# A four-layer graph network on one core: all arithmetic moved off GpSimd, to ScalarE and VectorE

## What is computed

```python
x = layernorm(x + L0(x))   # relu(adj @ (f1 * (adj @ (x @ W1)))) , then the same with W2 and f2, no relu
x = layernorm(x + L1(x))   # [x, adj @ x] @ weight
m = x @ W_msg + b_msg;  gates = sigmoid((m @ W_q) @ (m @ W_k).T / sqrt(128) + gate_bias) * adj * adj
u = relu([x, gates @ m] @ W_upd + b_upd);  x = layernorm(x + (layernorm(u) * ln_gamma + ln_beta))
x = layernorm(x + L3(x))   # z = swish(adj @ z @ W + b), twice
```

## Time and profile before

| what | value |
|---|---|
| device time, median of 3 runs | 1895.87 us (1895.03 to 1899.65) |
| span of the profiled execution | 1896.7 us |
| PE / DVE / ACT / POOL busy | 1683.2 / 1494.3 / 1007.3 / 471.2 us |
| busy share of the span | 89% / 79% / 53% / 25% |
| chain that ended last | PE 51%, DVE 34%, issue 9%, ACT 2%, POOL 1% |
| read from HBM | 420 MB, mean 223 GB/s |

### The profile page before, as it was taken

The page is one execution under the profiler, slowest core; times in us unless marked ns, Lnnn a source line. Parts: engine busy times, 40 slices in busy tenths (PEclk is TensorE's granted clock), DMA queues, the critical chain, the costliest instruction groups (busy, mean ns, idle before and its releaser), DMA issues.

```text
span 1896.7 us, 18699 instructions
## 1 busy us (share of the span) xinstructions
PE 1683.2 (89%) x7618; PEld 776.0 (41%) x7618; DVE 1494.3 (79%) x1231; ACT 1007.3 (53%) x709; POOL 471.2 (25%) x187
## 2 busy tenths in 40 slices
PE   7999999999999899898978786786786879999986
PEld 4444444444444444444433342242232434444432
DVE  6874565537556974788999999999999997654997
ACT  5764455446445543655646654554554756553753
POOL 1000000000000210112475656756756140000022
PEclk9999999999999999999989988888888999999999
DMA  9986776647766756666723433333333679764983
GB/s 374 391 315 232 258 312 248 240 176 285 268 243 230 280 206 239 246 246 240 266 89 133 149 118 111 118 126 111 112 132 111 240 252 353 286 232 171 351 304 139
DMA packets 59206, 423.64 MB, mean 223 GB/s; under 512 B 6800, under 2 KB 6960, under 8 KB 8304
## 3 DMA queue, kind: packets, MB, share of 16 engines
q1 hardware_dynamic: 57888, 417.88, 59.8%
q0 software_dynamic: 1088, 4.49, 0.7%
q10 hardware_dynamic: 144, 0.07, 0.0%
HBM read 420.32 MB, written 2.10 MB: 223 GB/s over the span
## 4 chain that ended last, share of the span: by engine, by line
PE 51%; DVE 34%; issue 9%; ACT 2%; POOL 1%; DMA 1%; SPq 0%; POOLq 0%; DVEq 0%; ACTq 0%
PE acc L502 32%; PE spare L502 15%; DVE gates L867 10%; DVE a_lo L851 9%; DVE a_lo L843 7%; ACT a_hi L677 2%; DVE bn L773 2%; PE rows L415 1%; PE rows L408 1%; DMA a_ring<-adj_dram 1%; DVE stats L784 1%; POOL x_rows L918 1%; DVE stats L787 1%; PE rows L421 1%; DVE moments L776 1%
## 5 line engine op out<-in xcount | busy, mean ns | idle before, releaser
L843 DVE SCALAR_TENSOR_TENSOR a_lo<-a_ring,a_hi 128x2048 f16<-128x2048 f32 x332 | 777.3, 2365 | 308.2 <-ACT a_hi L677 307.8
L677 ACT ACTIVATE a_hi<-a_ring 128x2048 f16<-128x2048 f32 x332 | 630.0, 1907 | 419.1 <-PE spare L502 275.1
L502 PE MATMUL acc<-a_hi,y_hi 128*128 128x512 f16 x1584 | 488.1, 390 | 157.9 <-DVE a_lo L851 121.4
L502 PE MATMUL acc<-a_hi,y_lo 128*128 128x512 f16 x1584 | 489.8, 391 | 0.0
L502 PE MATMUL acc<-a_lo,y_hi 128*128 128x512 f16 x1584 | 489.5, 391 | 0.0
L957 POOL TENSOR_TENSOR a_ring<-a_ring 128x1024 f32<-128x1024 f32 x112 | 312.1, 2813 | 97.2 <-DMA a_ring<-adj_dram 97.2
L909 POOL TENSOR_TENSOR val<-val,moments 128x1024 f32<-128x1024 f32 x19 | 51.2, 2694 | 1027.6 <-DVE moments L776 1027.6
L502 PEld LDWEIGHTS acc<-a_hi,y_hi 128*128 128x128 f16 x1584 | 150.2, 99 | 367.6 <-DVE a_lo L851 153.5
L685 ACT ACTIVATE a_hi<-gates 128x1024 f16<-128x1024 f32 x128 | 135.2, 1056 | 246.1 <-DVE gates L867 246.1
L851 DVE TENSOR_TENSOR a_lo<-gates,a_hi 128x1024 f16<-128x1024 f32 x128 | 263.5, 2058 | 0.0
L867 DVE SCALAR_TENSOR_TENSOR gates<-gates,a_ring 128x1024 f32<-128x1024 f32 x128 | 258.6, 2021 | 0.0
(11 more groups left out here) (111 smaller groups left out, 979.3 us busy)
## 6 DMA issues: line engine op xcount, KB each, us to landing
a_ring<-adj_dram SPq DMA_DIRECT2D x396, 1024.0 KB, 5.1
x_T<-xt_dram SPq DMA_DIRECT2D x4, 512.0 KB, 8.1
x_rows<-x_dram POOLq DMA_DIRECT2D x1, 2048.0 KB, 10.6
out_dram<-x_rows POOLq DMA_DIRECT2D x3, 512.0 KB, 4.6
out_dram<-x_rows SPq DMA_DIRECT2D x2, 256.0 KB, 2.0
w<-W_dram POOLq DMA_DIRECT2D x2, 64.0 KB, 5.4
wcat<-Wcat_dram POOLq DMA_DIRECT2D x1, 128.0 KB, 7.0
wupd<-W_upd_dram POOLq DMA_DIRECT2D x1, 128.0 KB, 7.6
```

The source lines that it names most:

```text
L502: mm = pe.matmul(sums[:, h * BANK:(h + 1) * BANK], blk(y[:, y_pass % 2, :], j), slot(a, st)[:, s, h * BANK:(h + 1) * BANK], start=(begins ...
L677: act.activation(slot(a_hi, st), loaded(st), ACT.Copy, scale=2.0 ** A_EXP).then_inc(s_ahi, 1)
L843: dve.scalar_tensor_tensor(out=slot(a_lo, st).rearrange("p s c -> p (s c)"), in0=loaded(st).rearrange("p s c -> p (s c)"), scalar=2.0 ** A ...
```

## The change

- The squares: ScalarE squares a whole step (128 x 2048) in one instruction, `square`. The first is issued ahead of the first sigmoid, and then one for the next step behind the second unit of each step. GpSimd squares nothing, and there is no eighth block of ScalarE's.
- The high halves: for units with u % 8 in (1, 4, 6) VectorE writes the high half by `tensor_copy`, directly behind low(u-1). The other five of eight stay on ScalarE. The two engines count on semaphores of their own.
- The layer norms: VectorE subtracts and scales in one instruction per block of 128 x 128, eight per norm (`normalise_blocks`), right behind the Newton steps or one or two units later. The norm with gain and offset takes sixteen (`normalise_affine`).
- The last chunk's halves are normalised by VectorE, four instructions each.
- GpSimd keeps the initial fill of the identity, its loads and the three stores.

```diff
@@ -32,7 +32,7 @@
 GATED = 6
 AHEAD = 4
 LONE_LOGITS = 5
-ACT_SQUARES = 8
+HIGH_BY_VECTOR = (1, 4, 6)
 
 
 A_EXP = 10
...
@@ -332,6 +332,19 @@
 
         def gated_index(st, s):
             return (st.n - GATED_FROM) * SJ + s
+
+        def high_by_vector(u):
+
+            return u % 8 in HIGH_BY_VECTOR
+
+        def highs_by_vector(u):
+
+            return sum(high_by_vector(v) for v in range(u))
+
+        def slot_free(u):
+
+            before = STREAM[GATED_FROM + u // SJ - RING]
+            return LAST_USE[before.n] + 1 - (SJ - 1 - u % SJ if before.p == GATED else 0)
 
         def in_idle_sums(u):
 
@@ -677,12 +690,16 @@
                 act.activation(slot(a_hi, st), loaded(st), ACT.Copy, scale=2.0 ** A_EXP).then_inc(s_ahi, 1)
 
             def gate_high(u):
+                if high_by_vector(u):
+                    return
                 st = STREAM[GATED_FROM + u // SJ]
                 act.wait_ge(s_g, u + 1)
-
-                before = STREAM[st.n - RING]
-                act.wait_ge(s_unit, LAST_USE[before.n] + 1 - (SJ - 1 - u % SJ if before.p == GATED else 0))
-                act.activation(slot(a_hi, st)[:, u % SJ, :], gates[:, u % G_RING, :], ACT.Copy).then_inc(s_ghi, 1)
+                act.wait_ge(s_unit, slot_free(u))
+                act.activation(slot(a_hi, st)[:, u % SJ, :], gates[:, u % G_RING, :], ACT.Copy).then_inc(s_ghi_act, 1)
+
+            def square(st):
+                act.wait_ge(s_a[st.n % LOADS], 16 * (st.n // LOADS + 1))
+                act.activation(loaded(st), loaded(st), ACT.Square).then_inc(s_sq, 1)
 
             for st in STREAM:
                 if st.p != GATED:
@@ -692,9 +709,8 @@
                 for s in range(SJ):
                     u = gated_index(st, s)
                     at = epilogue(stages, at, FIRST_USE[st.n] + s - AHEAD + 1)
-                    if u % ACT_SQUARES == ACT_SQUARES - 1:
-                        act.wait_ge(s_a[st.n % LOADS], 16 * (st.n // LOADS + 1))
-                        act.activation(loaded(st)[:, s, :], loaded(st)[:, s, :], ACT.Square).then_inc(s_sqa, 1)
+                    if u == 0:
+                        square(st)
                     act.wait_ge(s_lg, u + 1)
                     if u >= G_RING:
 
@@ -706,6 +722,8 @@
                                    scale=2.0 ** -(Q_EXP + K_EXP) * F ** -0.5).then_inc(s_pr, 1)
                     if u >= 1:
                         gate_high(u - 1)
+                    if s == SJ - 1 and u < NB * NC - 1:
+                        square(STREAM[st.n + 1])
                     if u == NB * NC - 1:
                         gate_high(u)
             epilogue(stages, at, THE_END)
...
@@ -811,6 +829,32 @@
                     rstd_of(range(CB), CB * n, n)
                 return go
 
+            def normalise_blocks(blocks, dst, n):
+
+                dve.wait_ge(s_newton, 3 * NEWTON * n)
+                for b in blocks:
+                    op = dve.tensor_scalar(dst(b), val[:, b, :], moments[:, b, 0:1], stats[:, 1, b:b + 1], ALU.subtract,
+                                           ALU.mult)
+                op.then_inc(s_ln, 1)
+
+            def normalise(run):
+                def go(p, k):
+                    normalise_blocks(range(CB), lambda b: normalised(p, k, run)[:, b, :], nth("ln", p, k, run))
+                return go
+
+            def normalise_affine(p, k):
+
+                n = nth("ln", p, k, 0)
+                dve.wait_ge(s_newton, 3 * NEWTON * n)
+                for b in range(CB):
+                    dve.scalar_tensor_tensor(out=xn[:, b, :], in0=val[:, b, :], scalar=moments[:, b, 0:1], in1=gam[:, :],
+                                             op0=ALU.subtract, op1=ALU.mult).then_inc(s_scaled, 1)
+                for b in range(CB):
+                    dve.wait_ge(s_scaled, CB * (nth("resid", p, k) - 1) + b + 1)
+                    op = dve.scalar_tensor_tensor(out=xn[:, b, :], in0=xn[:, b, :], scalar=stats[:, 1, b:b + 1],
+                                                  in1=bet[:, :], op0=ALU.mult, op1=ALU.add)
+                op.then_inc(s_ln, 1)
+
             def qk_low(run, hi, lo, exp):
                 def go(p, k):
                     i = ORDER[p][k]
@@ -826,15 +870,16 @@
                 1: {0: [take_over], 1: [values], 2: [y_low]},
                 2: {0: [take_over], 2: [y_low]},
                 3: {0: [take_over], 1: [values], 2: [y_low]},
-                4: {0: [take_over], 1: [values, ln_moments(0, s_val, "val"), ln_rstd(0)], 5: [y_low]},
-                5: {0: [take_over], 1: [values], 2: [ln_moments(0, s_val, "val"), ln_rstd(0)],
+                4: {0: [take_over], 1: [values, ln_moments(0, s_val, "val"), ln_rstd(0), normalise(0)], 5: [y_low]},
+                5: {0: [take_over], 1: [values], 2: [ln_moments(0, s_val, "val"), ln_rstd(0), normalise(0)],
                     7: [qk_low(0, kT_hi, kT_lo, K_EXP)], 8: [qk_low(1, qT_hi, qT_lo, Q_EXP)], 9: [y_low]},
-                6: {5: [values], 8: [ln_moments(0, s_nl, "nonlin")], 10: [ln_rstd(0)], 15: [residual],
-                    17: [ln_moments(1, s_res, "resid")], 20: [ln_rstd(1)], 23: [y_low]},
+                6: {5: [values], 8: [ln_moments(0, s_nl, "nonlin")], 10: [ln_rstd(0)], 12: [normalise_affine],
+                    15: [residual], 17: [ln_moments(1, s_res, "resid")], 20: [ln_rstd(1)], 21: [normalise(1)],
+                    23: [y_low]},
                 7: {2: [swish], 3: [y_low]},
-                8: {0: [take_over], 2: [swish], 4: [residual], 5: [ln_moments(0, s_res, "resid")], 6: [ln_rstd(0)]},
-                LAST_GATED: {2: [values], 4: [ln_moments(0, s_nl, "nonlin")], 5: [ln_rstd(0)], 8: [residual],
-                    10: [ln_moments(1, s_res, "resid")], 11: [ln_rstd(1)], 14: [y_low]},
+                8: {0: [take_over], 2: [swish], 4: [residual], 5: [ln_moments(0, s_res, "resid")], 6: [ln_rstd(0), normalise(0)]},
+                LAST_GATED: {2: [values], 4: [ln_moments(0, s_nl, "nonlin")], 5: [ln_rstd(0)], 6: [normalise_affine],
+                    8: [residual], 10: [ln_moments(1, s_res, "resid")], 11: [ln_rstd(1), normalise(1)], 14: [y_low]},
             }
             at = 0
 
@@ -845,9 +890,19 @@
                                          in1=slot(a_hi, st).rearrange("p s c -> p (s c)"), op0=ALU.mult,
                                          op1=ALU.subtract).then_inc(s_alo, 1)
 
+            def gate_high(u):
+                if high_by_vector(u):
+                    st = STREAM[GATED_FROM + u // SJ]
+                    dve.wait_ge(s_g, u + 1)
+                    dve.wait_ge(s_unit, slot_free(u))
+                    dve.tensor_copy(slot(a_hi, st)[:, u % SJ, :], gates[:, u % G_RING, :]).then_inc(s_ghi_dve, 1)
+
             def gate_low(u):
                 st = STREAM[GATED_FROM + u // SJ]
-                dve.wait_ge(s_ghi, u + 1)
+                if high_by_vector(u):
+                    dve.wait_ge(s_ghi_dve, highs_by_vector(u) + 1)
+                else:
+                    dve.wait_ge(s_ghi_act, u - highs_by_vector(u) + 1)
                 dve.tensor_tensor(slot(a_lo, st)[:, u % SJ, :], gates[:, u % G_RING, :], slot(a_hi, st)[:, u % SJ, :],
                                   ALU.subtract).then_inc(s_glo, 1)
 
@@ -860,15 +915,13 @@
                     u = gated_index(st, s)
                     at = epilogue(stages, at, FIRST_USE[st.n] + s - AHEAD + 1)
                     dve.wait_ge(s_pr, u + 1)
-                    if u % ACT_SQUARES == ACT_SQUARES - 1:
-                        dve.wait_ge(s_sqa, u // ACT_SQUARES + 1)
-                    else:
-                        dve.wait_ge(s_sq, u + 1 - u // ACT_SQUARES)
+                    dve.wait_ge(s_sq, u // SJ + 1)
                     dve.scalar_tensor_tensor(out=gates[:, u % G_RING, :], in0=gates[:, u % G_RING, :],
                                              scalar=2.0 ** G_EXP, in1=loaded(st)[:, s, :], op0=ALU.mult,
                                              op1=ALU.mult).then_inc(s_g, 1)
                     if u >= 1:
                         gate_low(u - 1)
+                    gate_high(u)
                     if u == NB * NC - 1:
                         gate_low(u)
             epilogue(stages, at, THE_END)
@@ -888,12 +941,18 @@
             def rstd_half(h):
                 rstd_of(range(h * HB, (h + 1) * HB), CB * last("ln", 0) + (h + 1) * HB, last("ln", h + 1))
 
+            def normalise_half(h):
+                first = ORDER[PASSES][NC - 1] * CB
+                normalise_blocks(range(h * HB, (h + 1) * HB), lambda b: x_rows[:, first + b, :], last("ln", h + 1))
+
             swish_half(0)
             moments_half(0)
             swish_half(1)
             rstd_half(0)
+            normalise_half(0)
             moments_half(1)
             rstd_half(1)
+            normalise_half(1)
 
 
         @block.gpsimd
@@ -903,41 +962,12 @@
             pool.affine_select(out=ident[:, :], in_=ident[:, :], compare_op=ALU.not_equal, fill=1.0, base=0,
```

(41 more changed lines are left out.)

28 lines of the change are left out of this document (5 added, 23 removed).

## The result

The changed kernel takes 1744.12 us (median of 4 runs, 1740.48 to 1744.6), the kernel before 1896.8 us beside it (median of 4). The ratio is 0.919, 95% interval 0.918 to 0.920: 8.1% faster. The forecast was 1729 us, the range 1690 to 1765 us. The profiled execution of the changed kernel has a span of 1738.7 us and is the fastest of its four; the others' spans are 1742.3 and 1742.8. In all four the time is 1.8 us longer than the span.

A forecast was written before the change was run, and what follows sets the result against it. VectorE, held by GpSimd's SBUF reads, was taken to bound the gated stage; 134 us off the stage and 33.4 us elsewhere, from 1896.7, gave 1729 us, range 1690 to 1765 us.

The forecast's parts named there:

- What binds the stage: Gated stage: VectorE is busy 555 of 558 us, and 214 us of that is contention with GpSimd.
- The rival on the other side: Gated stage: SBUF traffic of ScalarE and TensorE, not GpSimd, slows VectorE; stage 626 us, time about 1965 us; chance 0.03.
- The stage's sum: Gated stage: 354 us for 128 units, 50.7 other VectorE work, 16 norm arithmetic, 3 idling: 424 us in place of 558.
- The 48 copies: Gated stage: high halves written by VectorE, taken at 1.135 us each, 54.5 us in all.
- the rival by a page: Gated stage: copies take half their neighbours' time, 0.57 us each; stage 397 us, time 1705 us; chance 0.27.
- The norm instructions: Gated stage: layer-norm arithmetic moved to VectorE at 0.2 us per 128x128 operation, adding 16 us.
- the waits for ScalarE's order: Gated stage: VectorE waits 0.55 us for a sigmoid in one of four pairs of units, 9 us in all.
- theory B: From the follow-up experiments: VectorE waits for sigmoids because a chunk's first logits are made one after another in one buffer.
- ScalarE's order as a rival: Gated stage: the square between high half and next sigmoid makes each pair 6.1 us; 36 us more, 1765 us; chance 0.15.
- TensorE's clock: Gated stage: at a mean granted clock of 0.80 TensorE needs 442 us, 18 over the stage; time 1747 us; chance 0.10.
- Ahead of the stage: Passes 4 and 5: TensorE's waits go, 9.5 us for normalised chunks, 3 of low clock, 5.9 for low halves.
- Behind the stage: After the last gated chunk 7 us of low-half waits go, in pass 8 7 us, in the tail 1 us.

## Why the prediction was right

**What binds the stage.** Right, and shown by three runs: with the squares back on GpSimd the gain is gone, with reads that nobody needs VectorE is held, with writes alone it is not. The 214 us that I put down to contention went: gates and low halves average 1.217 us, for 2.02 and 2.06. One reading was too wide: the prediction had it that the slow ones are those that read only SBUF. The statistics read only SBUF too and never took over 0.296 us. The Trainium skill, "SBUF — State Buffer", section "Who interferes with whom", has VectorE and GpSimd share one pair of ports, which one of them holds for its whole instruction. By that rule a held instruction waits for the rest of the other one, and the runs agree: 1.7 and 0.20 us, the same for gate and copy. The rival on the other side (traffic of ScalarE and TensorE) falls by the same runs.

**The stage's sum: 424 forecast, 426 measured, by errors that cancel.** That it came so near is luck. Four terms were mis-sized. The 48 copies: I took 1.135 us each, 54.5; they cost 0.60, 29 us, so 26 less. (Against the run without them, VectorE's busy time is 26 us longer, 385.48 to 359.26.) This is the price of the rival by a page: the Trainium skill, "VectorE: DVE Perf Modes", section "The perf-mode tier table (the rule you actually need)", has a float32 copy at twice the rate of a tensor-tensor operation, and the trace agrees with 0.60 against 1.135. The norm instructions: I took 0.20 us from the statistics' rows; they cost 0.26, 80 of them 21 us for 16. It is not visible that those with one tensor (L836, 0.339 us) gain anything on those with two (L850, 0.343). The two splits of a step that the sum put into the stage, 4.5 us, don't run between its first gate and its last low half. And the waits for ScalarE's order: I gave 9 us and 3 of idling, and VectorE idled 40. So the work is 26 - 5 + 4.5 = 25.5 us less, and the idling 28 more.

Two of the prediction's own signs say this more plainly than its time does. VectorE was to be over 95% busy in the stage and is 90% (385.5 of 426); and over 30 us of idling released by the sigmoid, which it named as a sign of being wrong, did occur: 34.9 us. The rival by a page had its price right and its time wrong: at 1705 us it left out what VectorE would wait for once it was quick.

**What the 40 us are.** The prediction's sum was that of the steady state, where the order indeed costs little (1.3 us in the rest of the second chunk); it has no term for the starts of chunks. 17 us of the time hang on the squares in ScalarE's queue, and placing or cutting the pieces otherwise gives back 8. The other half can be read from the changed kernel's trace, though no run tests it. In the first chunk ScalarE's evacuation of pass 5's last sum (L613) stands in its queue ahead of a sigmoid and waits for TensorE's last product; at the start of each later chunk sixteen matmuls of TensorE's update projection (L428, 3.6 us) stand ahead of the next logits:

```profile
930.10 1.02 ACT L613 ACTIVATE z_T<-acc 128x1024 f32<-128x1024 f32 x1 [5.36 <-PE acc L515]
932.16 1.23 DVE L919 SCALAR_TENSOR_TENSOR gates<-gates,a_ring 128x1024 f32<-128x1024 f32 x1 [5.03 <-ACT gates L721]
...
1042.06 0.39 PE L428 MATMUL rows<-wupd,x_T 128*128 128x128 f32 x2
...
1045.63 0.59 PE L538 MATMUL acc<-qT_hi,kT_hi 128*128 128x512 f16 x2
1047.13 1.11 ACT L721 ACTIVATE gates<-acc,gbias 128x1024 f32<-128x1024 f32 x1 [3.61 <-PE acc L538]
1048.27 1.22 DVE L919 SCALAR_TENSOR_TENSOR gates<-gates,a_ring 128x1024 f32<-128x1024 f32 x1 [2.32 <-ACT gates L721]
```

The wait of 5.03 us is there in the run without squares too, and the one behind the projection as 3.05 and twice 2.66. So what remains of theory B is less the lone logits than what stands ahead of them. What would remove these waits I haven't tried.

**ScalarE's order as a rival** (36 us more than the sum) was right in mechanism and too high: ScalarE mostly has its lead. **TensorE's clock** as a rival was wrong: the clock rose to 0.97 as the long waits went, and the stage's 375.7 us of busy TensorE stay below VectorE's.

**Ahead of the stage: 18.4 forecast, 18.5 measured, and this too is luck.** The three waits of TensorE for a normalised chunk, 9.5 us, don't occur, as forecast. But in their place TensorE waits three times 1.1 us for a low half: the norm's instructions delay VectorE's next split, which the prediction had called covered. And pass 4's 5.9 us of waits for low halves, which were to go, are 5.9 us again. From 600 us to the stage's start those waits are, before and after:

```profile
PE acc L502 <- DVE a_lo L843: 9.0, 5, 2.8
...
PE acc L515 <- DVE a_lo L888: 11.7, 6, 3.4
```

The same stretch in the columns of the earlier trace rows:

```profile
600.00:935.00 335.00, 308.46 (x1454) 149.53 (x1453) 265.04 (x296) 181.48 (x111) 49.16 (x17) 0.97 0.70 255
600.00:916.50 316.50, 298.38 (x1441) 145.33 (x1439) 253.59 (x351) 182.05 (x111) 0.00 (x0) 0.99 0.73 269
```

TensorE's idling fell by 8.4 us (26.5 to 18.1). The other 10.1 us are its busy time, with a mean granted clock of 0.99 for 0.97. I estimate the clock's part at 7 us, from 335 x 0.03 less 316.5 x 0.01, where the forecast had 3.

**Behind the stage: 15 forecast, 7.1 measured.** This step failed in the total as well. Of the 13.5 us of waits for low halves after the last gated chunk 9.0 stay, and in pass 8 7.5 of 8.8, where I had 1.8:

```profile
PE acc L515 <- DVE a_lo L888: 9.0, 4, 3.7
...
PE acc L515 <- DVE a_lo L888: 7.5, 3, 2.6
```

And of the tail's 1 us 0.1 came: from TensorE's last transposes to the end it is 11.0 us before and 10.9 after. Behind the stage VectorE is busy 64.69 of 67.5 us: the norm's instructions that came to it (24 for that chunk, at 0.26) stand in its queue ahead of splits for which TensorE waits, and take the place of GpSimd's holding. The longest two of the waits, 3.64 and 3.71 us, end with the first splits behind them. The run with only the squares moved has 402.6 us behind its stage, that with the norms moved as well 397.2: the norms are worth 5.4 us there, 9.8 in the stage (445.3 to 435.5) and 14.3 ahead of it (933.1 to 918.8).

**The total.** The profiled executions differ by 158.0 us, the medians by 152.7. The profiled one after was the fastest of its four, 3.6 us under their median. The one before, at 1.8 us over its span of 1896.7, took 1898.5, which is 1.7 over its median; so the span does not stand 0.8 above the time, as I had it. The forecast of 167.4 was 9 us too much against the profiled difference: 1.6 in the stage, 8 behind it.

## What to carry to other kernels

Before moving work to GpSimd to relieve VectorE, look at VectorE's own instructions in the stretches where GpSimd runs: a minimum and a maximum that lie nearly one GpSimd instruction apart say that the two take turns, and the free engine costs more than it gives. Price the move by turns, which gives an upper bound: the GpSimd instructions that read SBUF (at most as many as VectorE has instructions that can be held) x the hold of one. In this stage that was 130 x 1.7 = 221 us before, where VectorE was busy some 220 us too long (555 - 385.5, and the 50 of copies and norms that came in), and 128 x 1.7 = 218 with the squares put back, where it was busy 187 us longer. And when the saturated engine gets quick, price the waits at the starts of chunks, not only the steady state.

## What was not expected of the hardware

- The two engines take turns: ten 128x128 instructions of GpSimd in 12.8 us beside nine or ten of VectorE's, each of which grew by 0.20 us and no more.
- The number of inputs doesn't decide what is held: the copy is, with one input (0.68 to 0.88 us); the statistics, also with one, are not (0.27 us in both); nor is an addition that reads one operand from PSUM (1.21 us in both).
- GpSimd's fills, busy 218 us of the stage, cost nothing but up to 0.09 us on some copies.
- A 128x128 instruction with two per-partition scalars costs 0.26 us from start to start, where statistics over the same 128 numbers cost 0.21 and a 128x1024 copy 0.60.
